# Conditioning by quarters in place, part of it in the block ahead, in an eight-block transformer kernel

## What is computed

```
def cond(x, side, w, u):          # r = x, k = v = side
    tf    = sigmoid(sum(cond_512, -1))
    decay = exp(-exp(w)) * (0.5 + 0.5 * tf)
    ek, ekv = exp(min(side, 30)), exp(min(side, 30)) * side
    num, den = forward and backward scans of ekv and ek, plus a bonus term with u
    return sigmoid(x) * (num / max(den, 1e-8)) * (0.8 + 0.2 * tf)
for block in blocks:
    x = x + block(cond(x, side, w_block, u_block))
```

## Time and profile before

| | us |
|---|---|
| median of 3 runs | 1317.99 (1313.64 to 1318.79) |
| profiled execution, whole | 1316.24 |
| profiled execution, span of the core's instructions | 1314.2 |
| PE busy | 1214.3 (92%) |
| DVE busy | 946.0 (72%) |
| ACT busy | 647.4 (49%) |
| POOL busy | 526.7 (40%) |

### The profile page before, as it was taken

How to read it: one execution, slowest core, us unless ns; L and a number is a source line. 1 busy time by engine, 2 the same in 40 slices (tenths; PEclk the granted TensorE clock), 3 DMA queues, 4 the chain that set the end, 5 groups by cost and what they waited for, 6 DMA issues and landing times. The chain is left out here.

```text
span 1314.2 us, 17066 instructions
## 1 busy us (share of the span) xinstructions
PE 1214.3 (92%) x5990; PEld 850.9 (65%) x5990; DVE 946.0 (72%) x1851; ACT 647.4 (49%) x1489; POOL 526.7 (40%) x424
## 2 busy tenths in 40 slices
PE   7989999999989989999799988999999986589997
PEld 2445656565567766343488866999999942268876
DVE  8877777776778986953643434999999989963354
ACT  3277677766655445446154325444444437053343
POOL 1068677666602321530073421555555520415520
PEclk9999999999989999999799998999999999799999
DMA  2122122111011102300544332111111010021111
GB/s 97 35 76 56 49 57 63 43 49 33 18 45 37 41 24 67 126 0 0 205 152 158 146 112 60 33 34 33 33 33 33 5 41 0 1 57 49 41 33 60
DMA packets 31508, 73.43 MB, mean 56 GB/s; under 512 B 5394, under 2 KB 15123, under 8 KB 28736
## 3 DMA queue, kind: packets, MB, share of 16 engines
q1 hardware_dynamic: 28848, 67.44, 16.6%
q0 software_dynamic: 1536, 3.86, 0.9%
q10 hardware_dynamic: 1040, 1.05, 0.2%
HBM read 55.89 MB, written 6.29 MB: 47 GB/s over the span
## 5 line engine op out<-in xcount | busy, mean ns | idle before, releaser
L179 POOL TENSOR_TENSOR sums<-scans 128x512 f32<-128x512 f32 x56 | 78.3, 1397 | 304.6 <-DVE scans L162 230.6
L574 POOL TENSOR_TENSOR probs<-probs,stats 128x512 f32<-128x512 f32 x64 | 83.8, 1309 | 107.9 <-DVE stats L743 107.9
L636 ACT ACTIVATE probs<-ps_s,stats 128x256 f32<-128x256 f32 (+1 forms) x256 | 104.3, 426 | 38.7 <-DVE stats L737 38.6
L199 DVE RECIPROCAL sums<-sums 128x256 f32<-128x256 f32 x56 | 98.1, 1752 | 1.8
L737 DVE CUSTOM_DVE_ANT_0 ps_s<-ps_s,mask 128x256 f32<-128x256 f32 (+1 forms) x256 | 83.1, 385 | 20.2 <-PE ps_s L868 20.2
L184 POOL TENSOR_TENSOR sums<-sums,terms 128x512 f32<-128x512 f32 x56 | 77.1, 1376 | 4.4
L2067 PE MATMUL K_ps_kvp<-K_wqkv_hi,K_xin_hi 128*128 128x256 f32 x256 | 75.1, 293 | 0.0
L1052 POOL TENSOR_TENSOR L3hid<-L3hid,L3sig 128x1024 f32<-128x1024 f32 x17 | 46.1, 2716 | 70.5 <-DVE L3hid L1178 37.8
L844 PE MATMUL ps_p<-xin,wkvq 128*128 128x512 f32 x144 | 70.1, 610 | 3.8 <-ACT qraw L625 1.8
L2067 PE MATMUL K_ps_kvp<-K_wqkv_hi,K_xin_lo 128*128 128x256 f32 x256 | 72.5, 283 | 0.0
L2067 PE MATMUL K_ps_kvp<-K_wqkv_lo,K_xin_hi 128*128 128x256 f32 x256 | 72.5, 283 | 0.0
(11 more groups left out here) (428 smaller groups left out, 3555.6 us busy)
## 6 DMA issues: line engine op xcount, KB each, us to landing
E_fc<-l_fc_dram SPq DMA_DIRECT2D x16, 1024.0 KB, 6.5
qswap<-qraw SPq DMA_DIRECT2D x60, 128.0 KB, 2.3
K_wqkv<-l_wqkv_dram SPq DMA_DIRECT2D x16, 384.0 KB, 3.3
L3wgu<-L_w_dram SPq DMA_DIRECT2D x17, 256.0 KB, 2.6
L0wgu<-L_w_dram SPq DMA_DIRECT2D x14, 256.0 KB, 2.6
L3wdn<-L_w_dram SPq DMA_DIRECT2D x17, 128.0 KB, 2.0
wkvq<-w_l0a_dram SPq DMA_DIRECT2D x4, 512.0 KB, 4.1
wo<-w_l0a_dram SPq DMA_DIRECT2D x4, 512.0 KB, 3.7
```

The costliest lines, as they stand in the source:

```text
L179: pstep.mark(pool.tensor_tensor(sums[:, k, :, :], scans[:, k, :, 0, :], scans[:, k, :, 1, :], ALU.add))
L199: dstep.mark(dve.reciprocal(den, den))
L574: pool.tensor_tensor(p1, p1, rs[:, 0:2].unsqueeze(2).to_broadcast([P, 2, T]), ALU.mult)
L636: ins = act.activation(dst[:, i % 2, :], src[:, i % 2, :], ACT.Exp, bias=stats[:, g % 4, 4 + i:5 + i], scale=-1.0, accum_out=stats[:, g % ...
```

## The change

1. **In place, by quarters.** The `sig` tiles go. A quarter's sigmoid is written into `xin` itself, and one DVE `tensor_tensor` of 128x512 multiplies it by `mod` there. `gain` is multiplied into `mod` where the quotient is made (L202, 56 times: `tensor_tensor` becomes `scalar_tensor_tensor`). Block 0 keeps the old form.
2. **Three sigmoids and two products in the block ahead.** Each add to `xT` of a quarter counts `x_added`; ACT follows with the sigmoid of quarters 0, 1, 2 and DVE multiplies quarters 0 and 1 ahead of its adds of quarter 3 and of the barrier. The next block starts with the sigmoid of quarter 3 and the products of quarters 2 and 3. The mixtures' last chunk counts `down_done` four times and is added by quarters. In L0 attention `next_sigmoid` moves ahead of the last evacuations.
3. **First weights a block ahead.** `w1`, `wqkv` pair 0 and the linear layer's `w` go into a kept tile (`ahead`), loaded at the end of the SP queue of an earlier block. The unread products at the start of R and F are taken out, and one of two at the end of E. In K the low part of pair 0 is made by DVE, and in the mixtures the first weight split comes behind the split of `xin`.
4. **Result by quarters.** Four stores of 256 KB, each behind its add, inside the last block. `stage_last` goes.

```diff
@@ conditioning
-    def condition_dve(dve, l, sig):
-        dstep.wait()
-        for h in range(2):
-            condition_half(dve, l, sig, h)
+    def quarter(x, n):
+        return x[:, n % 2, n // 2 * HALF:(n // 2 + 1) * HALF]
+    def quarter_act(act, l, n):
+        act.activation(quarter(xin, n), quarter(xT, n), ACT.Sigmoid).then_inc(sig_ready, 1)
+    def added_act(act, l, n):
+        act.wait_ge(x_added, ADDED[l - 1] + n + 1)
+        quarter_act(act, l, n)
+    def quarter_dve(dve, l, n):
+        if n == 0:
+            dstep.wait()
+        dve.wait_ge(sig_ready, 4 * l - 1 + n)
+        ins = dve.tensor_tensor(quarter(xin, n), quarter(xin, n), quarter(mod[:, l % 3], n), ALU.mult)
+        if n % 2:
+            ins.then_inc(xin_ready, 1)
@@ piece_quotient
-            dstep.mark(dve.tensor_tensor(part(mod[:, l % 3], i), sums[:, k, 0, :], den, ALU.mult))
+            dstep.mark(dve.scalar_tensor_tensor(out=part(mod[:, l % 3], i), in0=sums[:, k, 0, :], scalar=gain[:, i % NB:i % NB + 1],
+                                                in1=den, op0=ALU.mult, op1=ALU.mult))
@@ stage_l0_attn, end on ACT and on DVE
+                next_sigmoid(act, l + 1)
                 for g in (ALL - 3, ALL - 2, ALL - 1):
                     o_evac(g - 2)
                     pt_evac(g)
                 o_evac(ALL - 2)
                 o_evac(ALL - 1)
-                next_sigmoid(act, l + 1)
+                for n in range(3):
+                    act.wait_ge(s["wo_added"], 4 * L0_PAIRS + n + 1)
+                    quarter_act(act, l + 1, n)
...
                     wo_add(4 * L0_PAIRS + j + 1, j, ps_s[:, j // 2, 512 * (j % 2):512 * (j % 2) + 512])
+                    if j >= 2:
+                        quarter_dve(dve, l + 1, j - 2)
@@ stage_moe, SP, DVE and PE
+                if more:
+                    sp.dma_start(w1[:, :, :], io["l1_w1"]).then_inc(ld_w1, 16)
+                else:
+                    for n in range(4):
+                        sp.wait_ge(x_added, ADDED[l] + n + 1)
+                        sp.dma_start(quarter(io["yT"], n), quarter(xT, n)).then_inc(stored, 16)
+                    sp.wait_ge(stored, 64)
...
-                condition_act(act, sig)
-                gu_split(0)
+                quarter_act(act, l, 3)
...
-                after(dve, "down_done", NCH)
-                for ch in range(CH):
-                    x = xT[:, ch, :]
-                    dstep.link(dve.tensor_tensor(x, x, ps_y[:, ch, :, :].rearrange("p a t -> p (a t)"), ALU.add))
+                for n in range(4):
+                    after(dve, "down_done", NCH + n)
+                    x = quarter(xT, n)
+                    dve.tensor_tensor(x, x, ps_y[:, n % 2, n // 2, :], ALU.add).then_inc(x_added, 1)
+                    if more and n >= 2:
+                        quarter_dve(dve, l + 1, n - 2)
...
-                    ins.then_inc(s["down_done"], 1)
+                            if ch == NCH - 1:
+                                ins.then_inc(s["down_done"], 1)
@@ stage_l1_attn (R)
-                sp.dma_start(w1[:, :, :], io["l1_w1"]).then_inc(s["ld_w1"], 16)
-                sp.wait_ge(s["ld_w1"], 16)
...
-                unread_products(pe, ps[:, 7, :], 3)
-                pe.wait_ge(s["ld_w1"], 16)
+                pe.wait_ge(ld_w1, 16)
@@ stage_l1_ffn (E), end on PE
-                unread_products(pe, ps[:, 7, :], 2)
+                unread_products(pe, ps[:, 7, :], 1)
@@ stage_l2_attn (K), SP, POOL and DVE
+                sp.wait_ge(s["w_lo"], PAIRS - 2)
+                sp.dma_start(fw[:, :, :], io["l2_w"]).then_inc(ld_fw, 16)
...
-                split(0, 0, 0)
...
+                dve.wait_ge(s["w_hi"], 1)
+                dve.tensor_tensor(wqkv_lo[:, 0, :, :], wqkv[:, 0, :, :], wqkv_hi[:, 0, :, :], ALU.subtract)
...
+                quarter_dve(dve, l + 1, 0)
                 add(STEPS - 1, 1, 0)
+                quarter_dve(dve, l + 1, 1)
                 add(STEPS - 1, 1, 1, ps_q)
@@ stage_l2_ffn (F)
-                unread_products(pe, ps[:, 4, :], 2)
-                pe.wait_ge(s["ld_w"], 16)
+                pe.wait_ge(ld_fw, 16)
...
-                    if g == 1:
+                    if g == 0:
                         piece_finish(dve, l + 2, NP - 1, 1)
+                    if g >= 2:
+                        quarter_dve(dve, l + 1, g - 2)
```

More of the change, by code:

```diff
@@ L110, in build_program @@
     mod = keep("mod", [P, 3, CH, NT])
+    wqkv = keep("ahead", [P, 2, CH, 3 * P])
+    w1 = wqkv[:, 0, :, :]
+    fw = wqkv[:, 0, :, :].rearrange("p a b -> p (a b)")[:, 0:CH * C].rearrange("p (a b) -> p a b", a=CH)
     uk = keep("uk", [P, 2, T])
@@ L403, in _ @@
                 dstep.wait()
[L404 removed]
+                condition_half(dve, 0, xin, 0)
     stage_first()
@@ L1114, in _ @@
                     next_sigmoid(act, l + 1)
+                    for n in range(3):
+                        added_act(act, l + 1, n)
             @block.vector
@@ L2319, in _ @@
                     dve.wait_ge(s["done"], 12 + g + 1)
-                    x = xT[:, g % 2, half(g // 2)]
-                    dstep.mark(dve.tensor_tensor(x, x, ps[:, (12 + g) % 8, :], ALU.add))
+                    x = quarter(xT, g)
+                    dve.tensor_tensor(x, x, ps[:, (12 + g) % 8, :], ALU.add).then_inc(x_added, 1)
+                    if g >= 2:
+                        quarter_dve(dve, l + 1, g - 2)
             @block.tensor
```

111 lines of the change are left out of this document (61 added, 50 removed).

## The result

The changed kernel takes 1309.06 us (median of 7 runs, 1306.56 to 1312.45) against 1317.99 (median of 7, 1313.64 to 1320.89). The ratio is 0.994, with a 95% interval of 0.9926 to 0.9954: 0.6% faster, 8.9 us, where 11.3 were summed up and 1306 was forecast. It is inside the range of 1301 to 1312. A second set of six runs of it gave 1308.16 beside 1316.76 (0.9935, 0.9919 to 0.9952).

A forecast was written before the change was run, and what follows sets the result against it. PE was taken to bound most blocks, with waits at the seven barriers the place to gain. The terms summed to -11.3 us, 1304.9 for the profiled execution, 1306.7 on the median's scale; forecast 1306, range 1301 to 1312.

The forecast's parts named there:

- L0 attention's end: Boundary from L0 attention to the first mixture: the edit costs 1.8 us, from 0.6 to 2.2.
- first mixture to R: Barrier 0.45 us earlier and PE starting right behind it: 3.2 us less, or 2.2 if R's convolution inputs are late.
- E to K: Fewer unread products at E's end and earlier conditioning for K: 2.8 us less, from 0.8 to 4.4.
- gain in `mod`: 56 DVE instructions go from 423 to about 482 ns, 3.3 us in all; 0 on the path, 0 to 1.
- (a): L0 attention's end: the table load, now ahead of an evacuation PE needs, delays PE's end by some 1.15 us.
- (b): L0 attention's end: a product ahead of the last add and one behind it add 1.1 us.
- (c): First mixture's start: PE's wait of 0.35 us beyond its four unread products goes away, a gain of 0.35.
- The correction for the clock: K's start: no stand there, worth up to 1.6 us, against a later clock rise, up to 2.5 the other way.
- F and V: K's end to V: 4.1 us less, 2.5 of it from V's mixed input starting 1.4 behind PE instead of 3.9.
- The clock rival: Boundaries: PE stands longer and its clock falls or rises late, in the first mixture +3.4, K +1.7; 1311 us, chance 0.18.
- POOL against DVE: Product into `mod`: POOL and DVE disturb each other more; 0.6 us on each of 56 gives 33, 1339 us; chance 0.04.
- The edit does less than it says: R's start waits for convolution inputs, or K's for its second pair's split; 2 to 3 us lost, 1309; chance 0.14.

The follow-up runs named there:

- late_table: The changed kernel with the first attention's table load and its small activation back behind the last evacuations: 1305.28 us.
- w1_late: The changed kernel with R's first weights loaded inside R, as in the kernel before, conditionings still made ahead: 1312.72 us.
- store_quarters: The kernel before, with only the last mixture's adds and its store made by quarters: 1312.74 us.
- combined_a: The changed kernel with the edits of late_table, mixture_unread2, v_unread4 and f_unread4 together: 1304.9 us.
- v_unread4: The changed kernel with four in place of seven unread products at the start of V: 1306.28 us.
- f_unread4: The changed kernel with four in place of two unread products at F's end: 1307.37 us.
- mixture_unread2: The changed kernel with two in place of four unread products at the start of both mixtures: 1304.19 us.

## Why the prediction was right, point by point

The direction held and the time was inside the range, 3 us above the forecast. (The sum gives 1306.7 on the scale of the median, of which the forecast took 1306, and the end's own numbers, 1313.84 less 1310.4, give 3.4 and not 3.3.) By steps, with the size at like clock:

| step | forecast | measured |
|---|---|---|
| L0 attention's end | +1.8 | +1.93 (14.98 to 16.91) |
| first mixture to R | -3.2 | -2.9: barrier 0.9 earlier, R 2.0 shorter |
| R to E | 0 | 0: the first product 4.05 and 4.10 behind the barrier, released by a DMA |
| E to K | -2.8 | -4.05 at full clock (0.86 at E's end, 3.19 at K's start), some -1.2 to -2.3 where K begins at half |
| end of K | +0.5 | +0.49 |
| F (worked out in one sum with V) | -2.1 | -1.12 |
| V | -2.5 | -0.1 to -0.4, or -1.84 where it begins at full clock (both with +0.6 for the product ahead of the barrier) |
| gain in `mod` | 0 (0 to 1) | +1.2 |
| last mixture's start | +0.3 (+0.6 - 0.35) | the +0.6 is in V; the router starts 0.52 earlier, the length is within its spread |
| the end | -3.3 | -3.6 |

With V begun at half clock, as mostly, K at full, and 0.4 taken for the last mixture's start, the measured steps add up to some -8.7; by the medians it is -8.9. That they meet so closely is partly chance. The sum leaves out half clock in K, which six of twelve profiles of changed forms show, and what it does to the first mixture; the kernel before has some of it in K too (270.68 against 269.20). And that 1309 came out near 1306 owes something to luck: the forecast promised 1.2 us too little in E to K and 0.3 at the end, and too much in F (1.0), in `mod` (1.2) and in V (2.2).

**L0 attention's end.** The mechanism was right, the size too, with one offset: of (a), 0.98 arrive at ACT's last evacuation and 0.73 at the barrier (forecast 1.15), (b) is 1.20 (forecast 1.1). The 0.35 of (c) did not come, though it is in the +1.8: PE stood 2.06 ahead of the mixture and the unread products ran partly at half clock, so that the router started 5.22 behind the barrier in 8 of 9 profiles, 4.05 before. In late_table the activation starts 0.01 behind the end of the table load (366.55 + 1.28, then 367.84), as in the earlier trace rows, and the load's place costs 0.98 at most. The Trainium skill (ScalarE: Activation LUTs, What ACT_TABLE_LOAD costs) with its 2.66 would have made (a) 1.4 larger; the trace speaks against it here too.

**First mixture to R.** The barrier came 0.90 earlier relative to PE's last down product, twice the 0.45 of the forecast. PE began 0.17 behind it in place of 2.83, but then waited 0.44 for ACT's part of the convolution's inputs, and R kept 2.0. The forecast had named that wait, at 1 us, as a loss and as a sign against it. By the trace ACT came late since a `TENSOR_SCALAR` of DVE for the next block's quotient took 1.17 us (at 527.54) where it took 0.34 before. It now ran beside POOL's memsets, which fill the first 5 us of R in both kernels, and ACT waited 1.70 for it in place of 0.87. w1_late shows that both halves of the change are needed.

**E to K.** The correction for the clock was put at -2.5 to +1.6 and left at the middle. In store_quarters, where no half clock touches K in the form before, the first query product stood 7.18 behind the barrier; now it stands 3.99. The five unread products take 4.53 at full clock, and the 4.95 of the earlier trace rows, from which the forecast worked, held some half clock. With the 1.0 lost in K's middle and the 0.5 at its end this is 3.19 - 1.0 - 0.5 = 1.69, and K's lengths at full clock are 269.20 and 267.51. Where the half clock lasts 3.6 to 5.6 us into K, in six of twelve profiles of changed forms, K takes 269.3 to 270.4.

**F and V: the step that failed most.** F's first stretch fell from 5.3 to 2.3, in the range of the forecast (1.4 to 2.4) but not its middle of 2.0. The next instruction on DVE took 0.82 in place of 0.28 beside POOL's multiplication, the reciprocal waited for it, and F kept 1.1 of 2.1: the forecast had priced POOL's disturbance for the products alone. In V the term of 2.5 stands on unread products of 6.25, their price at full clock in the earlier trace rows, behind a stand of 0.99. The change made that stand 2.89, they ran at half clock and took 7.89, and the mixed input was there some 2.5 us ahead of PE (PE, waiting for it in combined_a, began at 5.25 behind the barrier, here at 7.75). What the text took as ending "about when the mixed input is there" was the bound: v_unread4 took 1.7 us out of V. The clock rival listed the longer stands ahead of the first mixture, F and the last mixture, and left this one out. Where V begins at full clock, the term was right: with the 0.6 for the product ahead of the next barrier counted apart, V got 2.44 shorter.

**The clock rival** was given 0.18 and a price of 5. It happened in part: at the first mixture +1.2 to the router, at V +1.6, in K 1.8 to 2.9 in half of the profiles. In V alone it took back 1.6 us of what full clock would give, and 3.4 to 4.5 with K where K has it too; whether the router's 1.2 reach the first mixture's end is not shown. Over the whole span the granted clock did not fall: 0.975 to 0.977 in the seven runs of the result, 0.971 to 0.978 in the runs of the kernel before, so half clock came at other places rather than for longer. f_unread4 shows that the part in V goes with how long PE stands, in 11 of 12 profiles of changed forms. That is what the Trainium skill (TensorE: Matmul & The Clock Gate, What's actually happening) says of an array left idle, and here the trace agrees: half clock at V's start in 8 of 9 profiles behind the long stand, in 0 of 3 behind the short one.

**Gain in `mod`.** 486 ns a piece, as the nearest row of 482 had it. That it costs nothing on the path failed: 0.4 us in the mixture, where DVE paces a part, and 0.7 in K. **POOL against DVE** did not decide the sign (its 33 us would need 0.6 for each of the 56 instructions), but the two disturbed instructions named above, neither of them the product into `mod`, cost 0.5 in F and, by the trace, 0.4 in R. **The edit does less than it says** came true by 0.6 in R only.

Of the signs for it, E's release by a DMA, the table load near 356 (357.94 and 355.48), K's first product right behind the unread ones, and four stores were seen; R's start came 0.17 behind the barrier, where 0.1 was named. Two of the three signs against it were seen as well: half clock in the first mixture's unread products, and R's first convolution waiting for ACT (0.44). By its own words the forecast was wrong in these two steps. The sum missed by 2.4 us, more by V, F and `mod` than by these.

The attention's 371.12 and 374.83 need a word: 1.78 of these 3.7 us stand ahead of the last probabilities, 1.04 of them already at PE's first product, which waits for a load (6.46 and 7.50). In v_unread4, late_table and mixture_unread2 that first product stands at 6.1 to 6.3, and the first block, with the attention unedited, spreads over 372.4 to 375.0 in nine profiles. It is the execution and not the edit, and it is 1.8 of the 2.9 us by which this pair of profiles (6.0 apart) falls short of the medians (8.9 apart).

## What to carry to other kernels

Work that only keeps an engine busy must be counted anew when the thing that it bridged gets shorter: in V, in the mixtures and in K the products that nobody reads had become the last thing ahead of useful work. When a stand is removed or made longer, look at the granted clock of the stretch behind it, and price the products there at both levels. And when a conditioning is moved ahead, its first weights have to move with it: in R the stand that was left without them cost more than was won.

## What the runs showed of the hardware

- The same program gave blocks that agree within 0.02 us where no half clock falls (R 112.00 to 112.02 in eleven profiles, F 11.84 or 11.85) and differ by up to 2.9 where it falls now and then (K 267.5 to 270.4). Much of the spread from execution to execution that shows by blocks goes with it. In the last mixture (157.86 to 159.36) this is not worked out: there it falls in every profile.
- A stand of 2.9 us ahead of V was followed by half clock in 8 of 9 profiles, one of 1.2 in none of 3. One of 3.3 inside the first mixture was followed by products of 0.63 us in place of 0.39, in four of four profiles that have it.
- A `TENSOR_SCALAR` of DVE over 128x256 took 1.17 us beside POOL's memsets where it took 0.34 behind them (R), and another 0.82 beside POOL's multiplication where it took 0.28 with POOL idle or done (F).
- A store of 1 MB behind 5 MB of loads took 11.9 us to land. With the last 2 MB held back it took 5.4 and no longer released the gather. And a quarter of the output landed in 2.5 where the whole took 3.9.
